# A fused attention and int8 feed-forward layer on eight cores: the weighted-sum matmuls trail the scores by six key blocks instead of four, and the weight transfers lose `single_packet`

## The chip, the cores and the metric

The kernel runs on all 8 cores of one Trainium2 chip. Every core runs the same program on its own share of the tokens, and there is no exchange between cores. The metric is the device time in microseconds of the slowest core, lower is better. A difference of 2% is about 63 us here.

## The reference, cut to what matters

```python
x = x + attn(layernorm(x), Wq, Wk, Wv, memory, memory_norm, memory_weight)   # 4 x 2048 x 2048
x = x + ffn(layernorm(x), w_gate, w_up, w_down, s_gate, s_up, s_down)

# attn: 32 query heads of 64, 8 key/value heads
probs = softmax(einsum('bsqhd,bthd->bqhst', qh, kh) / 8)
a_dot = einsum('bqhst,bthd->bsqhd', probs, vh)
sigma_q = elu(q);  a_mem = sigma_q @ memory / (sigma_q @ memory_norm)
out = a_dot * (1 - w) + a_mem * w                  # w = sigmoid(memory_weight)

# ffn: 2048 -> 8192 -> 2048, int8 weights with a scale per output column
out = ((silu((x @ w_gate) * s_gate) * ((x @ w_up) * s_up)) @ w_down) * s_down
```

Four sequences of 2048 tokens lie over eight cores: a core computes keys and values for a whole sequence (2048 tokens) and queries, attention and the feed-forward for 1024 of them.

## The kernel before, in words

The program is one function, `build_nc`. A small planner (`Plan.do`) appends each instruction to its engine's list in the order of the source and puts the semaphore waits in front of it; nothing is reordered, so the order of the loops is the order on each engine. `"t"` is TensorE, `"v"` VectorE, `"s"` ScalarE, `"y"` SyncE and `"g"` GpSimd. Every weight is loaded by a DMA that GpSimd issues, since it also casts (f32 or int8 in HBM, bf16 in SBUF); GpSimd waits for a buffer to come free, issues, and goes on.

1. Layer norm of the 16 token tiles and the projections: `wvb` (L179) is loaded once, the query weights in 16 pieces (L345), the key weights in 4 pieces twice (L361).
2. Then two passes `p` over 512 queries each. A pass has three stages.
   - Attention (L443 to L519). The loop `i2` runs over 16 pairs of heads. For each pair, 16 key blocks `tc` of 128 keys are worked through. A score step is two matmuls, L454 into `pAB` for one head and L461 into `pCD` for the other, each into one of two halves (`half`), so scores of block `tc` wait for the exponentials of block `tc - 2`. ScalarE then does two exponentials of 128 x 512 (L474) into `A_et`, a ring of 8 slots per head. The weighted sum of a block (L486, "AV" below: one matmul into `pE`, one into `pF`) is issued four steps after its scores; it accumulates over all 16 blocks. So the loop over `tc` has 20 steps: the first four have scores alone, the last four have AV alone. When the last AV is done, VectorE copies `pE` and `pF` out (L494, L498, L507, L514), and the first AV of the next pair waits for that. An exponential also waits for the AV that read its ring slot 8 blocks before.
   - The memory term and the sum of both (L528 to L648), mainly VectorE.
   - The feed-forward, for two groups `grp` of 256 tokens. First 64 steps `it` of gate (L698, 16 matmuls of 256 columns), up (L707, the same) and, two steps behind, the down projection of the group's first 128 tokens (L669, 4 matmuls of 512 columns). `wgb`, `wub` and `wdb` have two buffers each, and a step takes three transfers of 512 KB (written size): L688, L693, L663. Then the down projection of the second 128 tokens (L767), which reads all of `w_down` again through six buffers (L761), 64 transfers for 256 matmuls. These 64 steps are called the second down pass below; it comes four times in the program, as do the gate/up stages.

The first lines of the attention step's AV part:

```python
if tc >= 4:
    tca = tc - 4
    for st in range(2):
        ...
        waits=[t_exp[(j, tca)], war_av[st] if tca == 0 else None]
```

Of the kernel before, what the change touches and what calls it, by code (L numbers as in the profile page):

```python
# [59 lines left out]
def build_nc():  # L60
# [3 lines left out]
    wqt_d = nc.dram_tensor("wqt", [16, 128, 2048], F32, kind="ExternalInput").ap()  # L64
# [21 lines left out]
    with es:  # L86
# [72 lines left out]
        P = Plan()  # L159
# [16 lines left out]
            t_consts = P.do("y", lambda e, d=dst, s=src: e.dma_start(out=d[:], in_=s[:]), stream="c")  # L176
        t_mem = P.do("g", lambda e: e.dma_start(out=mem_s[:], in_=mem_d[:]), stream="m")
        t_mem = P.do("g", lambda e: e.dma_start(out=mnorm[:], in_=mnorm_d[:]), stream="m")
        t_wv = P.do("g", lambda e: e.dma_start(out=wvb[:], in_=wvt_d[:].rearrange("p (c f) -> p c f", f=512), single_packet=True), stream="wv")  # L179

        t_w1 = P.do("s", lambda e: e.activation(wcol[:, 0:1], mw_s[:], AF.Sigmoid),
                    waits=[t_consts], inc=True)
# [143 lines left out]
        for H in range(2):  # L326
            for i8 in range(8):
                i = H * 8 + i8
                sl = i % 2
                t_x[i] = P.do("y", lambda e, i=i, sl=sl: e.dma_start(  # L330
                    out=xstage[:, sl, :], in_=x_d[i * 128:(i + 1) * 128, :]),
                    waits=[war_xstage[sl]], stream="xs%d" % sl)
                tv3 = emit_ln_stats(xstage[:, sl, :], sl, [t_x[i]], war_lnst[sl],
                                    sum_on_s=True)
                if i8 > 0:
                    emit_tile_tail(i - 1)
                t_apply[i] = emit_ln_apply(xstage[:, sl, :], sl, tv3, eng="g")
                war_xstage[sl] = t_apply[i]
            emit_tile_tail(H * 8 + 7)
            t_half[H] = t_tile[H * 8 + 7]  # L340

            if H == 0:
                for j in range(16):
                    wb = j % 2
                    t_wq[j] = P.do("g", lambda e, j=j, wb=wb: e.dma_start(  # L345
                        out=wgb[wb][:], in_=wqt_d[j].rearrange("p (c m) -> p c m", m=128),
                single_packet=True),
                        waits=[war_wbuf[wb]], stream="wg%d" % wb)
                    for sc in range(2):
                        tv = qkv_group(  # L350
                            lambda c, j=j, wb=wb: wgb[wb][:, c, :],
                            lambda c, sc=sc: A_ln[:, c, sc * 512:(sc + 1) * 512],
                            lambda e, bank, j=j, sc=sc: e.tensor_copy(
                                q_fm[:, j, sc * 512:(sc + 1) * 512], bank[:, 0:512]),
                            16, [t_wq[j], t_tile[4 * sc + 3]])
                    t_q_evac[j] = tv
                    war_wbuf[wb] = ("t", P.cnt["t"])
                    norm_q_chunk(j)
            for j2 in range(4):
                wb = j2 % 2  # L360
                t_wk = P.do("g", lambda e, j2=j2, wb=wb: e.dma_start(  # L361
                    out=wgb[wb][:], in_=wkt_d[j2].rearrange("p (c m) -> p c m", m=128),
                single_packet=True),
                    waits=[war_wbuf[wb]], stream="wg%d" % wb)
                for tcH in range(2):
                    tv = qkv_group(
                        lambda c, wb=wb: wgb[wb][:, c, :],
                        lambda c, tcH=tcH: A_ln[:, c, tcH * 512:(tcH + 1) * 512],
                        lambda e, bank, j2=j2, H=H, tcH=tcH: e.tensor_copy(
                            k_fm[:, j2, H * 1024 + tcH * 512: H * 1024 + (tcH + 1) * 512],  # L370
                            bank[:, 0:512]),
                        16, [t_wk, t_tile[H * 8 + tcH * 4 + 3]])
                t_k_evac[(j2, H)] = tv
                war_wbuf[wb] = ("t", P.cnt["t"])
                norm_k_chunk(j2, H, tv)
            if H == 0:
                t_k0_done = ("t", P.cnt["t"])
            t_qkv_done[H] = ("t", P.cnt["t"])
# [37 lines left out]
        for p in range(2):  # L416
# [26 lines left out]
            for i2 in range(16):  # L443
                prs = (2 * i2, 2 * i2 + 1)
                kc = (2 * i2) % 8 // 2
                for tc in range(20):
                    if tc < 16:
                        half = (tc % 2) * 512
                        w0 = [t_exp.get((prs[1], tc - 2)), t_bias,
                              war_arena_p2]  # L450
                        if i2 == 0 and tc < 2:
                            w0 += war_sb_init[tc % 2]
                        ttSA = P.do("t", lambda e, i2=i2, kc=kc, tc=tc, half=half, p=p:
                                    e.matmul(pAB[0:128, half:half + 512],  # L454
                                             k_fm[0:64, kc, tc * 128:(tc + 1) * 128],
                                             q_fm[0:64, i2, p * 512:(p + 1) * 512],
                                             start=True, stop=True,
                                             tile_position=(0, 0)),
                                    waits=w0, inc=True)
                        ttSB = P.do("t", lambda e, i2=i2, kc=kc, tc=tc, half=half, p=p:  # L460
                                    e.matmul(pCD[0:128, half:half + 512],  # L461
                                             k_fm[64:128, kc, tc * 128:(tc + 1) * 128],
                                             q_fm[64:128, i2, p * 512:(p + 1) * 512],
                                             start=True, stop=True,
                                             tile_position=(64, 0)),
                                    inc=True)
                        for st in range(2):
                            j = prs[st]
                            wslot = t_av.get((j, tc - 8))
                            if wslot is None and i2 > 0:  # L470
                                wslot = t_av.get((j - 2, tc + 8))
                            t_exp[(j, tc)] = P.do(
                                "s", lambda e, j=j, tc=tc, st=st, half=half:
                                e.activation(A_et[:, st * 8 + tc % 8, :],  # L474
                                             sbank[st][0:128, half:half + 512],
                                             AF.Exp, bias=bias_s[:, j:j + 1],
                                             scale=0.125),
                                waits=[ttSB, t_bias, wslot,
                                       war_arena_p2], relax=True, inc=True)
                    if tc >= 4:  # L480
                        tca = tc - 4
                        for st in range(2):
                            j = prs[st]
                            t_av[(j, tca)] = P.do(
                                "t", lambda e, j=j, tca=tca, st=st:
                                e.matmul(avbank[st][0:65, 0:512],  # L486
                                         v_tm[:, tca, j % 8, 0:65],
                                         A_et[:, st * 8 + tca % 8, :],
                                         start=(tca == 0), stop=(tca == 15)),
                                waits=[t_exp[(j, tca)],  # L490
                                       war_av[st] if tca == 0 else None],
                                inc=True)
# [162 lines left out]
            for grp in range(2):  # L655
# [4 lines left out]
                def emit_down0(ic, grp=grp):  # L660
                    sl = ic % 2
                    buf = wdb[sl]
                    t_wd = P.do("g", lambda e, ic=ic, buf=buf: e.dma_start(  # L663
                        out=buf[:], in_=wd_d[ic * 128:(ic + 1) * 128, :],
                        single_packet=True),
                        waits=[ttdn0.get(ic - 2), war_wd[sl] if ic < 2 else None],
                        stream="wd%d" % sl)
                    for dch in range(4):
# [14 lines left out]
                for it in range(64):  # L683
                    wb = it % 2
                    wu_extra = [t_qkv_done[1]] if (p == 0 and grp == 0 and it < 2) else []
                    if it < 2:
                        wu_extra = wu_extra + [war_wu_reg[wb]]
                    t_wg = P.do("g", lambda e, it=it, wb=wb: e.dma_start(  # L688
                        out=wgb[wb][:], in_=wg_d[it], single_packet=True),
                        waits=[war_wbuf[wb]] +  # L690
                              ([war_wg_reg[wb]] if it < 2 else []),
                        stream="wd%d" % (4 + wb) if False else "wg%d" % wb)
                    t_wu = P.do("g", lambda e, it=it, wb=wb: e.dma_start(  # L693
                        out=wub[wb][:], in_=wu_d[it], single_packet=True),
                        waits=[war_wbuf[wb]] + wu_extra, stream="wu%d" % wb)
                    ttg = None
                    for c in range(16):
# [60 lines left out]
                for ic in range(64):  # L758
                    sl = ic % 6
                    buf = wd_slots[sl]  # L760
                    t_wd = P.do("g", lambda e, ic=ic, buf=buf: e.dma_start(  # L761
                        out=buf[:], in_=wd_d[ic * 128:(ic + 1) * 128, :],
                        single_packet=True),
                        waits=[ttdn.get(ic - 6), war_wd6[sl] if ic < 6 else None],
                        stream="wd%d" % sl)
                    for dch in range(4):
# [127 lines left out]
```

How the kernel before makes its waits and increments, by code:

```python
            def run(eng):  # L801
                for item in stream:
                    if item[0] == "w":
                        eng.wait_ge(sems[item[1]], item[2])
                    elif item[0] == "i":
                        item[1](eng).then_inc(sems[item[2]], STEP[item[2]])
                    else:
                        item[1](eng)
```

## Time and profile before

| what | us |
|---|---|
| median of the runs shown (two: 3134.87 and 3320.86) | 3227.86 |
| the profiled execution | 3137.72 |
| its span, first to last instruction of the slowest core (core 3) | 3136.2 |
| spans of the eight cores | 3120.4 to 3136.2 |
| core 3: one attention stage of 16 head pairs (two in the program) | about 326 |
| core 3: one second down pass of 64 steps (four in the program) | about 82 |

Rows of the profile are in microseconds from the span's start unless they say ns. PE is TensorE's matmuls, PEld its weight loads, DVE VectorE, ACT ScalarE, POOL GpSimd, SP SyncE. A row of the timeline reads: start, duration, engine, line, operation, what is written <- what is read, count, and in brackets how long the engine was idle before and what ended that. Matmuls overlap: what one costs is the distance between two starts, not its duration.

### The profile page before, as it was taken

How to read it: one execution, taken by the hardware profiler on the slowest of the kernel's cores; microseconds unless marked ns; L12 is line 12 of the kernel's file. 1: busy time of each engine (PE TensorE's matmuls, PEld its weight loads, DVE VectorE, ACT ScalarE, POOL GpSimd, SP SyncE). 2: the span in 40 equal slices, each digit the busy share in tenths (PEclk: the TensorE clock that was granted, in tenths of full speed). 3: DMA queues.
4: the chain of work that ended last, by engine and by line, in shares of the span. 5: the costliest groups of instructions: out<-in, count | busy, mean ns of one | idle time of the engine just before them, and what ended most of it. 6: DMA issues, size and time to landing. Idle time of an engine off the chain costs nothing.

```text
span 3136.2 us, 40984 instructions; the slowest of 8 cores (3120.4 to 3136.2 us)
## 1 busy us (share of the span) xinstructions
PE 2445.5 (78%) x14265; PEld 1329.0 (42%) x14265; DVE 595.7 (19%) x1657; ACT 963.5 (31%) x1671; POOL 590.6 (19%) x1071
## 2 busy tenths in 40 slices
PE   3777666878744799968999778875449997799986
PEld 1223222222211577725778222221127774277752
DVE  2332333111136200020000011112550002000010
ACT  2200030999920122201222059995002221022210
POOL 1100010000000233323333310000003332333333
PEclk9788778888855799989999988887559998999999
DMA  4222214000000599979999960000009996999999
GB/s 116 74 44 44 44 65 121 4 4 4 4 1 1 187 358 359 350 280 366 357 348 361 361 218 4 3 4 3 1 28 353 351 354 248 395 339 361 349 338 346
DMA packets 161916, 591.77 MB, mean 189 GB/s; under 512 B 20920, under 2 KB 23096, under 8 KB 157368
## 3 DMA queue, kind: packets, MB, share of 16 engines
q0 software_dynamic: 151344, 552.14, 51.5%
q1 hardware_dynamic: 10376, 37.01, 3.4%
q8 instruction: 124, 2.03, 0.3%
q14 instruction: 72, 0.59, 0.1%
HBM read 325.23 MB, written 8.39 MB: 106 GB/s over the span
## 4 chain that ended last, share of the span: by engine, by line
PE 56%; DMA 12%; DVE 12%; ACT 11%; issue 8%; DVEq 1%; SPq 0%; POOL 0%; ACTq 0%; POOLq 0%
PE pAB L707 13%; PE pAB L698 13%; ACT arena L474 9%; DMA warena<-wd 8%; PE pCD L296 5%; PE pAB L296 4%; PE pCD L669 3%; PE pE L486 3%; PE pAB L454 3%; DMA warena<-wg 2%; PE pF L486 2%; PE pAB L571 2%; PE pT L238 2%; PE pF L669 2%; PE pE L669 2%
## 5 line engine op out<-in xcount | busy, mean ns | idle before, releaser
L698 PE MATMUL pAB<-ln_fm,warena 128*128 128x256 bf16 x4096 | 493.7, 274 | 13.4 <-DMA warena<-wg 11.1
L707 PE MATMUL pAB<-ln_fm,warena 128*128 128x256 bf16 x4096 | 490.0, 273 | 10.3 <-DMA warena<-wu 6.1
L688 POOL DMA_DIRECT2D warena<-wg x256 | 136.2, 532 | 1733.0 <-PE pAB L698 1037.2
L698 PEld LDWEIGHTS pAB<-ln_fm,warena 128*128 128x128 bf16 x4096 | 398.6, 98 | 125.6 <-issue 41.9
L707 PEld LDWEIGHTS pAB<-ln_fm,warena 128*128 128x128 bf16 x4096 | 399.3, 98 | 63.9 <-issue 16.9
L474 ACT ACTIVATE arena<-pAB,bias_s 128x512 bf16<-128x512 f32 x512 | 373.2, 729 | 46.1 <-PE pCD L461 41.9
L474 ACT ACTIVATE arena<-pCD,bias_s 128x512 bf16<-128x512 f32 x512 | 375.5, 733 | 0.0
L454 PE MATMUL pAB<-q_fm,k_fm 64*128 64x512 bf16 x512 | 217.2, 434 | 134.7 <-ACT arena L474 129.8
L714 ACT ACTIVATE gtmp<-pAB,sg_s 128x256 bf16<-128x256 f32 x256 | 121.4, 474 | 567.1 <-PE pAB L707 504.1
L722 DVE TENSOR_TENSOR arena<-gtmp,utmp 128x256 bf16<-128x256 bf16 x256 | 75.0, 293 | 1063.8 <-ACT utmp L718 1063.8
L486 PE MATMUL pE<-arena,v_tm 128*65 128x512 bf16 x512 | 228.0, 445 | 0.0
L461 PE MATMUL pCD<-q_fm,k_fm 64*128 64x512 bf16 x512 | 222.2, 444 | 0.0
L718 ACT ACTIVATE utmp<-pAB,su_s 128x256 bf16<-128x256 f32 x256 | 121.4, 474 | 321.9 <-PE pAB L707 318.9
L767 PE MATMUL pCD<-warena,arena 128*128 128x512 bf16 x512 | 158.4, 390 | 77.6 <-DMA warena<-wd 65.9
L486 PE MATMUL pF<-arena,v_tm 128*65 128x512 bf16 x512 | 216.8, 423 | 0.0
L238 PE MATMUL pT<-eyeb_s,lnstage 128*128 128x128 bf16 x384 | 78.2, 248 | 167.4 <-DVE arena L241 68.3
L454 PEld LDWEIGHTS pAB<-q_fm,k_fm 64*128 64x128 bf16 x512 | 46.1, 95 | 370.7 <-issue 370.7
L761 POOL DMA_DIRECT2D warena<-wd x256 | 135.5, 531 | 250.4 <-PE pF L767 151.0
L669 PE MATMUL pCD<-warena,arena 128*128 128x512 bf16 x512 | 153.1, 381 | 16.1 <-DMA warena<-wd 15.7
L663 POOL DMA_DIRECT2D warena<-wd x256 | 141.6, 553 | 37.8 <-PE pAB L698 16.4
L693 POOL DMA_DIRECT2D warena<-wu x256 | 139.4, 544 | 41.3 <-PE pF L279 16.3
L494 DVE CAST arena<-pE 64x512 bf16<-64x512 f32 x32 | 21.9, 683 | 560.3 <-PE pE L486 560.3
(118 smaller groups left out, 2074.4 us busy)
## 6 DMA issues: line engine op xcount, KB each, us to landing
warena<-wd POOLq DMA_DIRECT2D x512, 512.0 KB, 6.0
warena<-wg POOLq DMA_DIRECT2D x256, 512.0 KB, 3.9
warena<-wu POOLq DMA_DIRECT2D x256, 512.0 KB, 4.8
xstage<-x SPq DMA_DIRECT2D x16, 1024.0 KB, 5.0
warena<-wqt POOLq DMA_DIRECT2D x16, 512.0 KB, 5.2
x<-x SPq DMA_DIRECT2D x8, 1024.0 KB, 13.5
y<-x SPq DMA_DIRECT2D x8, 1024.0 KB, 4.7
warena<-wkt POOLq DMA_DIRECT2D x8, 512.0 KB, 5.2
```

What stands on the lines that cost most here:

```text
L238: tt = P.do("t", lambda e, c=c, ap=ap: e.transpose(ap, lnstage[:, slot, c * 128:(c + 1) * 128], eyeb[:]), waits=[t_apply, tslot_war[si]] + ...
L296: tt = P.do("t", lambda e, c=c, bank=bank: e.matmul(bank[:, 0:512], lhs_fn(c), rhs_fn(c), start=(c == 0), stop=(c == nK - 1)), waits=(wait ...
L454: e.matmul(pAB[0:128, half:half + 512], k_fm[0:64, kc, tc * 128:(tc + 1) * 128], q_fm[0:64, i2, p * 512:(p + 1) * 512], start=True, stop=True,
L461: e.matmul(pCD[0:128, half:half + 512], k_fm[64:128, kc, tc * 128:(tc + 1) * 128], q_fm[64:128, i2, p * 512:(p + 1) * 512], start=True, st ...
L474: e.activation(A_et[:, st * 8 + tc % 8, :], sbank[st][0:128, half:half + 512], AF.Exp, bias=bias_s[:, j:j + 1], scale=0.125),
L486: e.matmul(avbank[st][0:65, 0:512], v_tm[:, tca, j % 8, 0:65], A_et[:, st * 8 + tca % 8, :], start=(tca == 0), stop=(tca == 15)),
L663: t_wd = P.do("g", lambda e, ic=ic, buf=buf: e.dma_start(out=buf[:], in_=wd_d[ic * 128:(ic + 1) * 128, :], single_packet=True), waits=[ttd ...
L669: ttdn0[ic] = P.do("t", lambda e, ic=ic, buf=buf, dch=dch: e.matmul(dbanks[dch][0:128, 0:512], A_fu[:, ic, 0:128], buf[:, dch * 512:(dch + ...
L693: t_wu = P.do("g", lambda e, it=it, wb=wb: e.dma_start(out=wub[wb][:], in_=wu_d[it], single_packet=True), waits=[war_wbuf[wb]] + wu_extra, ...
L698: ttg = P.do("t", lambda e, it=it, wb=wb, c=c: e.matmul(pA[0:128, 0:256], wgb[wb][:, c, :], ln2_fm[:, c, 0:256], start=(c == 0), stop=(c = ...
L707: ttu = P.do("t", lambda e, it=it, wb=wb, c=c: e.matmul(pB[0:128, 0:256], wub[wb][:, c, :], ln2_fm[:, c, 0:256], start=(c == 0), stop=(c = ...
L767: ttdn[ic] = P.do("t", lambda e, ic=ic, buf=buf, dch=dch: e.matmul(dbanks[dch][0:128, 0:512], A_fu[:, ic, 128:256], buf[:, dch * 512:(dch ...
```

## The change

Two things. In the attention loop AV trails the scores by six steps instead of four: the loop has 22 steps, the first six with scores alone and the last six with AV alone. And the flag `single_packet=True` is taken off all weight transfers (`wvb`, L345, L361, L663, L688, L693, L761: 1,049 DMAs); what they move, who issues them and what they wait for stays.

```diff
-        t_wv = P.do("g", lambda e: e.dma_start(out=wvb[:], in_=wvt_d[:].rearrange("p (c f) -> p c f", f=512), single_packet=True), stream="wv")
+        t_wv = P.do("g", lambda e: e.dma_start(out=wvb[:], in_=wvt_d[:].rearrange("p (c f) -> p c f", f=512)), stream="wv")
...
-                for tc in range(20):
+                for tc in range(22):
...
-                    if tc >= 4:
-                        tca = tc - 4
+                    if tc >= 6:
+                        tca = tc - 6
...
                     t_wg = P.do("g", lambda e, it=it, wb=wb: e.dma_start(
-                        out=wgb[wb][:], in_=wg_d[it], single_packet=True),
+                        out=wgb[wb][:], in_=wg_d[it]),
...
                     t_wu = P.do("g", lambda e, it=it, wb=wb: e.dma_start(
-                        out=wub[wb][:], in_=wu_d[it], single_packet=True),
+                        out=wub[wb][:], in_=wu_d[it]),
...
                     t_wd = P.do("g", lambda e, ic=ic, buf=buf: e.dma_start(
-                        out=buf[:], in_=wd_d[ic * 128:(ic + 1) * 128, :],
-                        single_packet=True),
+                        out=buf[:], in_=wd_d[ic * 128:(ic + 1) * 128, :]),
```

The change moves instructions on TensorE alone. The first place is the start of a head pair other than the first. In the kernel before, TensorE has this order from the fourth score step on (`k_fm` and `q_fm` are keys and queries, `arena` holds the exponentials, `v_tm` the values):

```order
L454 MATMUL pAB<-q_fm,k_fm 128x512 [waits sem_s]
L461 MATMUL pCD<-q_fm,k_fm 128x512
L454 MATMUL pAB<-q_fm,k_fm 128x512 [waits sem_s]
L461 MATMUL pCD<-q_fm,k_fm 128x512
L486 MATMUL pE<-arena,v_tm 65x512 [waits sem_v]
L486 MATMUL pF<-arena,v_tm 65x512 [waits sem_v]
```

In the changed kernel, from the same score step on (L454 is L452 there, L461 is L459, L486 is L484):

```order
L452 MATMUL pAB<-q_fm,k_fm 128x512 [waits sem_s]
L459 MATMUL pCD<-q_fm,k_fm 128x512
L452 MATMUL pAB<-q_fm,k_fm 128x512 [waits sem_s]
L459 MATMUL pCD<-q_fm,k_fm 128x512
L452 MATMUL pAB<-q_fm,k_fm 128x512 [waits sem_s]
L459 MATMUL pCD<-q_fm,k_fm 128x512
L452 MATMUL pAB<-q_fm,k_fm 128x512 [waits sem_s]
L459 MATMUL pCD<-q_fm,k_fm 128x512
L484 MATMUL pE<-arena,v_tm 65x512 [waits sem_v]
L484 MATMUL pF<-arena,v_tm 65x512 [waits sem_v]
```

The first AV, which waits for VectorE's copies of the pair before, comes behind two more score steps.

The second place is the end of a head pair: the last score step, the AVs behind it and the first score matmul of the next pair. Before:

```order
L454 MATMUL pAB<-q_fm,k_fm 128x512 [waits sem_s]
L461 MATMUL pCD<-q_fm,k_fm 128x512
L486 MATMUL pE<-arena,v_tm 65x512
L486 MATMUL pF<-arena,v_tm 65x512
...
L486 MATMUL pE<-arena,v_tm 65x512 [waits sem_s]
L486 MATMUL pF<-arena,v_tm 65x512 [waits sem_s]
L486 MATMUL pE<-arena,v_tm 65x512 [waits sem_s]
L486 MATMUL pF<-arena,v_tm 65x512 [waits sem_s]
L454 MATMUL pAB<-q_fm,k_fm 128x512
```

In the changed kernel, where the "..." also stands for rows like the two above it:

```order
L484 MATMUL pE<-arena,v_tm 65x512
L484 MATMUL pF<-arena,v_tm 65x512
...
L484 MATMUL pE<-arena,v_tm 65x512 [waits sem_s]
L484 MATMUL pF<-arena,v_tm 65x512 [waits sem_s]
L484 MATMUL pE<-arena,v_tm 65x512 [waits sem_s]
L484 MATMUL pF<-arena,v_tm 65x512 [waits sem_s]
L452 MATMUL pAB<-q_fm,k_fm 128x512
```

Between the last score matmul (L461) and the next pair's first (L454) stood 10 AV matmuls, and now 14 stand there. The last four wait for ScalarE in both.

## Rows read from the trace of the kernel before

**Rows 1.** The page: busy time of each engine, and the granted clock in 40 slices

```profile
PE 2445.5 (78%) x14265; PEld 1329.0 (42%) x14265; DVE 595.7 (19%) x1657; ACT 963.5 (31%) x1671; POOL 590.6 (19%) x1071
PEclk9788778888855799989999988887559998999999
```

**Rows 2.** The page: the chain that ended last, by line

```profile
PE pAB L707 13%; PE pAB L698 13%; ACT arena L474 9%; DMA warena<-wd 8%; PE pCD L296 5%; PE pAB L296 4%; PE pCD L669 3%; PE pE L486 3%; PE pAB L454 3%; DMA warena<-wg 2%; PE pF L486 2%; PE pAB L571 2%; PE pT L238 2%; PE pF L669 2%; PE pE L669 2%
```

**Rows 3.** Windows: stretch and length, busy us (instructions) by engine, granted clock, DMA share, GB/s

```profile
545.40:872.20 326.80, 259.93 (x1020) 72.28 (x1020) 41.14 (x60) 303.44 (x513) 0.00 (x0) 0.85 0.02 4
648.50:668.10 19.60, 14.39 (x66) 4.44 (x64) 2.76 (x5) 18.63 (x33) 0.00 (x0) 1.00 0.02 5
671.15:677.98 6.83, 6.17 (x18) 1.24 (x18) 0.00 (x0) 6.19 (x11) 0.00 (x0) 0.50 0.03 7
```

**Rows 4.** Timeline around the end of one head pair

```profile
645.36 0.37 PE L454 MATMUL pAB<-q_fm,k_fm 64*128 64x512 bf16 x1 [0.21 <-ACT arena L474]
...
645.68 0.41 PE L486 MATMUL pE<-arena,v_tm 128*65 128x512 bf16 x1
...
646.71 0.81 ACT L474 ACTIVATE arena<-pCD,bias_s 128x512 bf16<-128x512 f32 x1
...
647.43 0.38 PE L486 MATMUL pE<-arena,v_tm 128*65 128x512 bf16 x1
647.67 0.38 PE L486 MATMUL pF<-arena,v_tm 128*65 128x512 bf16 x1
...
647.98 0.39 PE L454 MATMUL pAB<-q_fm,k_fm 64*128 64x512 bf16 x1
...
648.50 0.69 ACT L474 ACTIVATE arena<-pAB,bias_s 128x512 bf16<-128x512 f32 x1 [0.97 <-PE pCD L461]
```

**Rows 5.** Timeline of VectorE: the copy that ends a head pair, three in a row

```profile
647.92 0.68 DVE L494 CAST arena<-pE 64x512 bf16<-64x512 f32 x1 [17.51 <-PE pE L486]
...
667.50 0.68 DVE L494 CAST arena<-pE 64x512 bf16<-64x512 f32 x1 [16.54 <-PE pE L486]
...
688.22 0.68 DVE L494 CAST arena<-pE 64x512 bf16<-64x512 f32 x1 [17.67 <-PE pE L486]
```

**Rows 6.** Timeline: first AV of a pair, score steps at half and at full clock

```profile
672.34 0.64 PE L486 MATMUL pE<-arena,v_tm 128*65 128x512 bf16 x1
...
674.88 0.60 PE L454 MATMUL pAB<-q_fm,k_fm 64*128 64x512 bf16 x1
...
676.41 0.60 PE L454 MATMUL pAB<-q_fm,k_fm 64*128 64x512 bf16 x1
...
682.19 0.37 PE L454 MATMUL pAB<-q_fm,k_fm 64*128 64x512 bf16 x1 [0.21 <-ACT arena L474]
...
683.34 0.37 PE L454 MATMUL pAB<-q_fm,k_fm 64*128 64x512 bf16 x1 [0.21 <-ACT arena L474]
```

**Rows 7.** The second down pass: its DMA issues (duration in ns), and one PE row

```profile
L761 POOL DMA_DIRECT2D warena<-wd x58: 527/527/539, 1366.1 to 1439.5; - x58
...
1437.96 0.59 PE L767 MATMUL pCD<-warena,arena 128*128 128x512 bf16 x2 [0.26 <-DMA warena<-wd]
```

**Rows 8.** DMA issues of the page: KB each, median us from issue to landing

```profile
warena<-wd POOLq DMA_DIRECT2D x512, 512.0 KB, 6.0
...
warena<-wkt POOLq DMA_DIRECT2D x8, 512.0 KB, 5.2
...
mem_s<-memi POOLq DMA_DIRECT2D x1, 512.0 KB, 6.3
```

**Rows 9.** Gate/up stage: a wg transfer's issue, matmuls of two steps, and median landing

```profile
1103.79 0.53 POOL L688 DMA_DIRECT2D warena<-wg  x1 [2.77 <-PE pCD L669]
...
1103.95 1.91 PE L698 MATMUL pAB<-ln_fm,warena 128*128 128x256 bf16 x16
...
1108.30 1.91 PE L698 MATMUL pAB<-ln_fm,warena 128*128 128x256 bf16 x16
...
warena<-wg POOLq DMA_DIRECT2D x22, 512.0 KB, 3.7
```

More of the change, by code:

```diff
@@ L345, in build_nc @@
                     t_wq[j] = P.do("g", lambda e, j=j, wb=wb: e.dma_start(
-                        out=wgb[wb][:], in_=wqt_d[j].rearrange("p (c m) -> p c m", m=128),
-                single_packet=True),
+                        out=wgb[wb][:], in_=wqt_d[j].rearrange("p (c m) -> p c m", m=128)),
                         waits=[war_wbuf[wb]], stream="wg%d" % wb)
@@ L361, in build_nc @@
                 t_wk = P.do("g", lambda e, j2=j2, wb=wb: e.dma_start(
-                    out=wgb[wb][:], in_=wkt_d[j2].rearrange("p (c m) -> p c m", m=128),
-                single_packet=True),
+                    out=wgb[wb][:], in_=wkt_d[j2].rearrange("p (c m) -> p c m", m=128)),
                     waits=[war_wbuf[wb]], stream="wg%d" % wb)
@@ L663, in emit_down0 @@
                     t_wd = P.do("g", lambda e, ic=ic, buf=buf: e.dma_start(
-                        out=buf[:], in_=wd_d[ic * 128:(ic + 1) * 128, :],
-                        single_packet=True),
+                        out=buf[:], in_=wd_d[ic * 128:(ic + 1) * 128, :]),
                         waits=[ttdn0.get(ic - 2), war_wd[sl] if ic < 2 else None],
@@ L761, in build_nc @@
                     t_wd = P.do("g", lambda e, ic=ic, buf=buf: e.dma_start(
-                        out=buf[:], in_=wd_d[ic * 128:(ic + 1) * 128, :],
-                        single_packet=True),
+                        out=buf[:], in_=wd_d[ic * 128:(ic + 1) * 128, :]),
                         waits=[ttdn.get(ic - 6), war_wd6[sl] if ic < 6 else None],
```

## The prediction, made before the changed kernel ran

> **What bounds the kernel now.** I read the page first, then the chain, and then the stages that the change touches one by one. The busy shares [rows 1] say little by themselves: TensorE is busy 78% of the span, but that is a mean over stages with different limits. The clock digits already show that there is something to look for: in the slices of attention (8 to 11 and 24 to 28 of 40) TensorE is granted 0.7 to 0.8 of its clock, 0.85 as the mean of the first stage [rows 3], not the full one. The chain [rows 2] names the parts: gate and up matmuls 26%, the exponentials of attention (L474) 9%, and transfers of w_down 8%, some 250 us. So the two edits touch two different bounds. The later AV touches a stage in which ScalarE leads, and the flag touches a stage that waits for DMA.
>
> **Attention, the bound inside a head pair.** At the full clock a step takes 683.34 - 682.19 = 1.15 us [rows 6], and TensorE was idle 0.21 us before its scores, released by ScalarE: ScalarE's two exponentials set the pace. Within a pair that ran at the full clock ScalarE was busy 18.63 of 19.60 us [rows 3]. What is left, about 1 us, is the hole at the pair's end [rows 4]: ScalarE starts its last exponential at 646.71, and the first of the next pair starts at 648.50, after 0.97 us of idleness ended by a score matmul. Who fills the time between? TensorE starts the last score at 645.36, its first AV at 645.68 and the ninth at 647.43. That is 1.75 us for 8 matmuls, 0.219 each, with no gap; the tenth follows at 647.67 and the next pair's scores at 647.98. The last exponential ended at 647.52 (646.71 + 0.81), before the tenth AV started. So the tail behind the last score is bound by the number of matmuls that stand in it, not by the exponentials, although it is close: 0.15 us.
>
> **The tail, first term.** The change puts four more AV matmuls behind the last score (14, not 10). All AVs that were deferred have their exponentials ready, so nothing hides them: during them ScalarE finishes its last two steps, as before, and then it has no scores to work on. The steps before cannot absorb them either, since TensorE runs its list in order. Cost per pair: 4 x 0.219 = 0.88 us; for 2 x 16 pairs 28 us. The bound from below is the 0.15 us that might be covered if I misread the end of the last exponential: 32 x 0.73 = 23 us. From above, at half the clock a 512-column matmul would cost twice as much, 56 us, but the tail stood at the full clock in the pairs I looked at: the half-clock stretch is early in the pair, 671.15 to 677.98 [rows 3], after the copy at 667.50 and before the one at 688.22 [rows 5]. I take 28.
>
> What else the six steps could wait for: an exponential needs its ring slot free, that is the AV of 8 blocks before. With a delay of 6 that AV is issued two steps before the exponential, ahead of the exponential's own scores on the same engine, so it adds no wait. The first AV of a pair waits for VectorE's copies; it comes two steps later now, which can only help, and nothing was waiting there.
>
> **The clock, second term.** The period of a pair is read from the copies that end it [rows 5]: 19.58 us for the pair that the second row ends, 20.72 for the next. The difference is the clock. The first pair was granted 1.00 throughout, the second 0.50 (1.2 GHz) from 671.15 to 677.98 [rows 3]. In that stretch a step takes 676.41 - 674.88 = 1.53 us instead of 1.15 [rows 6], since two scores together and two AVs at half speed are more than two exponentials. The fall comes after a stretch in which TensorE had only scores to do. The whole first stage has 16 pairs in about 325.5 us (326.8 less 1.3 around it), 20.34 each, or 0.76 above 19.58; two stages lose 32 x 0.76 = 24 us to the clock.
>
> What do two more steps with scores alone do to this? Steps without AV do not suffer from the half clock. If the low stretch stayed where it is, it would fall on steps without AV, and up to 24 us would come back; that is the lower bound, -24. But the rise at 677.98 came only after AVs had run for 5.6 us (the first AV of that pair starts at 672.34 [rows 6]); if the rise follows the AVs, it moves two steps too, and the same three slow steps stand there, later. The pairs that now escape the fall would no longer do so, since the light stretch is longer. The upper bound is two more slow steps per pair, 32 x 2 x 0.38 = +24. I take +6, nearer to "it moves along" than to either end.
>
> The Trainium skill's page "TensorE: Matmul & The Clock Gate", in "Part 1: The HAM clock gate", says that the throttled state is the default and that activity releases it. The trace agrees: 0.50 follows the steps with scores alone. By this rule the longer light stretch makes the low clock certain in every pair, and does not by itself shorten it.
>
> **The flag, third term.** Nothing is moved on GpSimd's list, no byte is added and no wait changes. What the flag could touch is how fast a transfer runs, how long it takes to land, and how long GpSimd takes to issue it. The second down pass is where it would show at once: 58 issues from 1366.1 to 1439.5 [rows 7], 1.29 us for each 512 KB or 407 GB/s, while TensorE's 4 matmuls of 512 columns need 4 x 0.219 = 0.88 us. It waits for the DMA in each step, 0.26 us in the row shown. Four passes of 64 steps are 330 us, and each per cent of transfer rate is 3.3 us. The gate/up stage has a step of 1108.30 - 1103.95 = 4.35 us [rows 9] for three transfers, 3 x 1.29 = 3.87 us at that rate: 11% in hand. Of latency there is less in hand: wg issued at 1103.79 is wanted at 1108.30, 4.51 us later, and lands after 3.7, which leaves 0.8.
>
> No row shows the same transfer with and without the flag. The nearest is mem_s, a 512 KB casting load that never had it: 6.3 us to landing against 5.2 for the key weights that had it [rows 8], with a cold start and the small constants beside it. So the upper bound: 1.1 us later landing in all. In gate/up 1.1 - 0.8 = 0.3 us a step, 256 steps, 77 us; in the second down pass six buffers are in flight (6 x 1.29 = 7.7 us against 6.0 + 1.1 to land), little more, say 15: +92 us. The lower bound is a pass that no longer waits: 256 x (1.29 - 0.88) = -105 us, if the DMA were suddenly that fast. Both are far off. I take the value of the rows in which each descriptor's work is unchanged, one per cent of the passes, +3 us.
>
> The Trainium skill's page "DMA: Bandwidth & Descriptors", in "Why small descriptors are slow (HBM only)", gives a packet a fixed overhead of about 3 cycles beside one cycle per 32 bytes, and says that packing descriptors together is only worth it up to 256 bytes. The rows here have 4 KB written per partition; by the page that is 3 in 131 cycles, an estimate of 2.3%, or 8 us of 330. No row of this trace shows it. With it the sum would be 5 us higher.
>
> **The sum.** The profiled execution took 3137.7 us, 1.5 more than its span. 3137.7 + 28 + 6 + 3 = 3174.7, so 3175 us, 1.2% above it. The median of the two runs shown is 3227.86, between 3134.87 and 3320.86; my sum stands to the lower of them, which the profiled execution matches within 3 us. A difference of 2% is about what a measurement of this kernel can tell from no change.
>
> **The rivals.**
> *A, not slower: the clock pays for the tail.* The half-clock stretch comes where it comes now, over steps that no longer have AVs, and is over when they begin. Then the 24 us are gained back against the 28 of the tail: 3137.7 + 28 - 24 + 0 = 3142. For it: the fall comes early, about 3.6 us after the pair's end. Against it: the rise followed the AVs. It decides if the granted clock rises before the seventh step.
> *B, the rate drops.* Transfers lose 10%: the second down passes go from 1.29 to 1.42 us a step, +33, while gate/up still hides it (3 x 1.42 = 4.26 under 4.35). 3137.7 + 34 + 33 = 3205. For it: those passes have no reserve. Against it: nothing in rows says that splitting costs as much.
> *C, the landing gets later.* The upper bound above, 3137.7 + 34 + 92 = 3264. For it: mem_s, and only 0.8 us in hand at wg. Against it: mem_s was the first transfer of all.
> *D, the flag does nothing.* If the transfers were cut the same way in both kernels, only attention moves: 3172. It is inside my forecast.
>
> **How the numbers follow.** Forecast, D included, 0.66; A 0.12; B 0.12; C 0.10. The forecast by itself spans 3155 to 3195 (first term 23 to 28, second -5 to +20, third 0 to 10, and a few us of scatter). The range is 3143 to 3212: it takes in B and most of A and leaves C and a part of A out. 2% above 3137.7 is 3200.5: slower by over 2% is C, half of B and a little of the forecast's upper edge, 0.17. Faster by over 2% would need the lower bound of the flag, 0.03. Within 2%: 0.80.
>
> **What would show it.** Right, step by step: ScalarE's idle time before the first exponential of a pair grows from 0.97 to about 1.85 us; pairs at the full clock take 20.4 to 20.5 us between copies; nearly every pair has a stretch at 0.50, which ends some 2 us later in the pair than now; an attention stage takes about 343 us instead of 326. The second down pass keeps 1.29 us a step, and wg still lands within 4 us in gate/up. The prediction is wrong if the attention stage stays within 5 us of 326 (A, or a tail that is hidden), or if the steps of the second down pass or the landing times grow by more than 3% (B, C).

## The result, and the profile after

The changed kernel takes 3166.31 us (median of 11 runs) against 3142.67 us for the kernel before (median of 10). The ratio to the kernel before is 1.0083, with a 95% interval of 1.0070 to 1.0097: 26 us slower. The ratio leaves out the executions in which the cores of a die showed a lower granted clock and took over 1% longer (three of the 10, one of the 11), so it gives 26 us where the two medians lie 24 apart. The prediction was 3175 us, 1.2% above the profiled execution of before (3137.7). It set aside the median of two runs, 3227.86 us, that was shown before it, and nothing below goes by that either.

Against the profiled execution the sign and the place were right; the size was 37 us where 26 came. The page of the profile after first, whose slowest core is core 4:

```profile
span 3166.1 us, 40808 instructions; the slowest of 8 cores (3142.4 to 3166.1 us)
...
PEclk8788867788865699989999988887559998999999
...
PE pAB L704 14%; PE pAB L695 13%; ACT arena L472 9%; DMA warena<-wd 8%; PE pCD L296 5%; PE pAB L296 5%; PE pE L484 3%; PE pCD L666 3%; PE pAB L452 3%; PE pF L484 3%; PE pAB L569 2%; DMA warena<-wg 2%; PE pT L238 2%; PE pF L666 2%; PE pE L666 2%
```

The chain has the same members with the same shares as [rows 2]: the transfers of w_down are at 8% in both. The page cannot tell where 26 us went. The two stages of attention can. In windows of core 4 (length, busy us of PE, PEld, DVE, ACT and POOL, granted clock, DMA share, GB/s):

```profile
557.50:896.10 338.60, 257.80 (x1019) 74.68 (x1018) 41.15 (x60) 303.29 (x513) 0.00 (x0) 0.83 0.02 4
...
669.70:676.50 6.80, 6.18 (x18) 1.24 (x18) 0.00 (x0) 6.15 (x11) 0.00 (x0) 0.50 0.01 2
...
1857.10:2195.00 337.90, 257.36 (x1018) 74.71 (x1019) 44.55 (x65) 303.01 (x513) 0.00 (x0) 0.83 0.07 23
```

Each stage is about 338 us long, 326.8 before [rows 3], with the same busy time of ScalarE (303 us). ScalarE is not slower, it waits more. The clock is granted at 0.83 instead of 0.85. The end of a pair in the timeline, to be held beside [rows 4]:

```profile
660.30 0.37 PE L452 MATMUL pAB<-q_fm,k_fm 64*128 64x512 bf16 x1 [0.21 <-ACT arena L472]
...
660.63 0.41 PE L484 MATMUL pE<-arena,v_tm 128*65 128x512 bf16 x1
...
661.67 0.80 ACT L472 ACTIVATE arena<-pCD,bias_s 128x512 bf16<-128x512 f32 x1
...
663.46 0.38 PE L484 MATMUL pF<-arena,v_tm 128*65 128x512 bf16 x1
...
663.77 0.39 PE L452 MATMUL pAB<-q_fm,k_fm 64*128 64x512 bf16 x1
...
664.29 0.69 ACT L472 ACTIVATE arena<-pAB,bias_s 128x512 bf16<-128x512 f32 x1 [1.82 <-PE pCD L459]
```

From the last score at 660.30 the 14 AVs run without a gap to 663.46, and ScalarE, whose last exponential started at 661.67, is idle 1.82 us until the next pair's first scores: 0.97 before. In what follows "the hole" is the distance between the start of a pair's last exponential and the start of the next pair's first, here 664.29 - 661.67 = 2.62 us. Inside a stretch of exponentials the same distance is 0.57. The hole of before [rows 4] is 648.50 - 646.71 = 1.79.

The transfers show nothing. The issues of the second down pass (as in [rows 7]), the median landing of wg in gate/up (as in [rows 9]), and from the page the pieces in which the weight queue moved its data:

```profile
L758 POOL DMA_DIRECT2D warena<-wd x52: 527/527/530, 1400.3 to 1465.6; - x52
```

```profile
warena<-wg POOLq DMA_DIRECT2D x22, 512.0 KB, 3.9
```

```profile
DMA packets 161916, 591.77 MB, mean 187 GB/s; under 512 B 20920, under 2 KB 23096, under 8 KB 157368
## 3 DMA queue, kind: packets, MB, share of 16 engines
q0 software_dynamic: 151344, 552.14, 50.9%
```

65.3 us for 51 steps is 1.28 us a step, 1.29 before. And wg lands after 3.9 us in the stretch where it was 3.7; over the eight cores it is 3.7 to 3.9 in both. The number of pieces is the same as before, where the page has 161916 in all and 151344 on this queue too.

One table holds what the later sections use. Each value is worked out from the starts of all exponentials in the timelines of all eight cores (of the run with three steps, cores 0 to 3 alone): the hole as the mean of 30 per core, and "within a pair" as the time from its first exponential to its last, the mean of 32 per core. At the full clock throughout, within a pair would be 15 steps of 1.145 us and one distance of 0.57, 17.75 us. Whatever is above that is lost to the half clock.

| kernel | AV matmuls behind the last score | first AV at step | hole, us | within a pair, us | ratio to before |
|---|---|---|---|---|---|
| two steps | 6 | 2 | 1.84 | 18.15 | 0.9965 (0.9950 to 0.9980) |
| three steps | 8 | 3 | 1.83 | 18.21 | 0.9979 (0.9948 to 1.0009) |
| before, four steps | 10 | 4 | 1.79 | 18.63 | 1 |
| five steps | 12 | 5 | 2.18 | 18.31 | 1.0016 (1.0001 to 1.0031) |
| changed kernel, six steps | 14 | 6 | 2.60 | 18.59 | 1.0083 (1.0070 to 1.0097) |
| seven steps | 16 | 7 | 3.01 | 18.62 | 1.0139 (1.0115 to 1.0163) |
| late start, short tail | 10 | 6 | 1.87 | 18.65 | 1.0004 (0.9991 to 1.0017) |
| early start, long tail | 14 | 4 | 2.64 | 18.29 | 1.0046 (1.0031 to 1.0061) |
| pipelined | none | 6 | 0.57 | 18.28 | 0.9843 (0.9825 to 0.9862) |
| pipelined, five steps | none | 7 | 0.57 | 18.23 | 0.9829 (0.9806 to 0.9852) |

Steps are counted from 0 in this table, as `tc` is. The changed kernel against the one before: hole +0.81, within a pair -0.04. With 30 holes and 32 pairs that is 23 us. The tail behind the last pair of each of the two stages is not followed by a hole in this count; at the same price, an estimate, it adds 2 us, so that 25 of the 26 us have their place.

### The profile page after: what moved, and what is told of

It is laid out like the page before. It is cut to its first block, busy times and chain, and to the rows that moved or that the text cites. A ratio compares the mean times of both kernels' runs of the same rounds, so it can differ in the third digit from the quotient of the medians.

```text
span 3166.1 us, 40808 instructions; the slowest of 8 cores (3142.4 to 3166.1 us)
## 1 busy us (share of the span) xinstructions
PE 2427.0 (77%) x14089; PEld 1336.0 (42%) x14265; DVE 595.7 (19%) x1657; ACT 962.0 (30%) x1671; POOL 590.6 (19%) x1071
## 2 busy tenths in 40 slices
DMA packets 161916, 591.77 MB, mean 187 GB/s; under 512 B 20920, under 2 KB 23096, under 8 KB 157368
## 3 DMA queue, kind: packets, MB, share of 16 engines
q0 software_dynamic: 151344, 552.14, 50.9%
## 4 chain that ended last, share of the span: by engine, by line
PE 57%; DVE 11%; DMA 11%; ACT 11%; issue 8%; DVEq 1%; SPq 0%; ACTq 0%; POOL 0%; POOLq 0%
PE pAB L704 14%; PE pAB L695 13%; ACT arena L472 9%; DMA warena<-wd 8%; PE pCD L296 5%; PE pAB L296 5%; PE pE L484 3%; PE pCD L666 3%; PE pAB L452 3%; PE pF L484 3%; PE pAB L569 2%; DMA warena<-wg 2%; PE pT L238 2%; PE pF L666 2%; PE pE L666 2%
## 5 line engine op out<-in xcount | busy, mean ns | idle before, releaser
L452 PE MATMUL pAB<-q_fm,k_fm 64*128 64x512 bf16 x512 | 222.7, 445 | 164.1 <-ACT arena L472 157.0
L459 PE MATMUL pCD<-q_fm,k_fm 64*128 64x512 bf16 x512 | 228.2, 456 | 0.0
L484 PE MATMUL pE<-arena,v_tm 128*65 128x512 bf16 x512 | 223.3, 436 | 0.0
L763 PE MATMUL pCD<-warena,arena 128*128 128x512 bf16 x500 | 155.2, 389 | 81.1 <-DMA warena<-wd 68.1
L484 PE MATMUL pF<-arena,v_tm 128*65 128x512 bf16 x512 | 215.9, 422 | 0.0
L452 PEld LDWEIGHTS pAB<-q_fm,k_fm 64*128 64x128 bf16 x512 | 46.4, 95 | 397.8 <-issue 397.8
L666 PE MATMUL pCD<-warena,arena 128*128 128x512 bf16 x388 | 125.9, 380 | 21.6 <-DMA warena<-wd 15.1
```

The lines of the kernel that those rows point to most:

```text
L452: e.matmul(pAB[0:128, half:half + 512], k_fm[0:64, kc, tc * 128:(tc + 1) * 128], q_fm[0:64, i2, p * 512:(p + 1) * 512], start=True, stop=True,
L459: e.matmul(pCD[0:128, half:half + 512], k_fm[64:128, kc, tc * 128:(tc + 1) * 128], q_fm[64:128, i2, p * 512:(p + 1) * 512], start=True, st ...
L484: e.matmul(avbank[st][0:65, 0:512], v_tm[:, tca, j % 8, 0:65], A_et[:, st * 8 + tca % 8, :], start=(tca == 0), stop=(tca == 15)),
L666: ttdn0[ic] = P.do("t", lambda e, ic=ic, buf=buf, dch=dch: e.matmul(dbanks[dch][0:128, 0:512], A_fu[:, ic, 0:128], buf[:, dch * 512:(dch + ...
L763: ttdn[ic] = P.do("t", lambda e, ic=ic, buf=buf, dch=dch: e.matmul(dbanks[dch][0:128, 0:512], A_fu[:, ic, 128:256], buf[:, dch * 512:(dch ...
```

## The experiments

### The two edits apart

The later AV alone, from the kernel before:

```diff
-                for tc in range(20):
+                for tc in range(22):
...
-                    if tc >= 4:
-                        tca = tc - 4
+                    if tc >= 6:
+                        tca = tc - 6
```

> The later weighted sum alone; single_packet stays on all weight transfers. Theory T (the four further AV matmuls in each pair's tail carry the whole loss, the flag nothing): as the changed kernel, ratio to before 1.008 (within 0.002), hole before a pair's first exponential 2.6 us between starts. Rival F (the flag has a share, the tail less): ratio clearly under the changed kernel's 1.0083, for a share of a third 1.0055. Rival G (the flag's removal gave some time back): ratio over 1.010.

Measured: ratio 1.0066 (1.0049 to 1.0083), hole 2.60 us, within a pair 18.58. By the trace the attention stages are those of the changed kernel (336.3 us from the first to the last exponential's start against 336.5, the mean over eight cores, and 324.9 in the kernel before). The ratio alone would leave room for a small share of the flag. So the flag alone, the changed kernel with the loop of before:

```diff
-                        out=wgb[wb][:], in_=wg_d[it], single_packet=True),
+                        out=wgb[wb][:], in_=wg_d[it]),
```

and likewise at all other weight transfers, so that against the kernel before only the flag differs.

> The flag alone: no single_packet on any weight transfer, AV four steps behind as before. Theory T: ratio 1.000 within 0.0015, the second down pass at 1.29 us a step and 407 GB/s, wg landing 3.7 to 3.9 us after issue in gate/up. Rival F: ratio 1.003 or more (8 us), seen as a longer step of the second down pass, since it waits for its transfers in every step. Rival G: ratio under 0.998.

Measured: ratio 1.0004 (0.9992 to 1.0015), hole 1.79 us. The second down pass on core 0 of this run:

```profile
L758 POOL DMA_DIRECT2D warena<-wd x39: 527/527/530, 1399.6 to 1449.2; - x39
...
DMA to landing us min/median/max: 6.0/6.0/6.9
```

49.6 us for 38 steps, 1.305 us, with a landing of 6.0 us as in [rows 8] and 527 ns for an issue as in [rows 7]. One pass on one core is a small sample; from the seventh to the last issue, over all four passes and eight cores, the step is 1.300 us before and 1.297 us in this run. This is the stage that waits for its transfers in every step, so a slower or later transfer could not hide here. Rivals F and G are out: the flag is worth nothing that can be measured, between -2.5 and +4.7 us (0.08% and 0.15% of 3138).

### Late start or long tail

The change did two things in each pair: the first AV came later, and more AVs stood behind the last score. The next two kernels do one each, by a table that says which blocks' AVs stand at a step.

```diff
-                    if tc >= 4:
-                        tca = tc - 4
-                        for st in range(2):
+                    for tca in AVS[tc]:
+                        for st in range(2):
```

Late start, short tail: one AV pair a step from step 6 on, two at steps 12 and 14, so that the last four steps are those of before.

> From the kernel before: the first AV of a pair comes at the seventh step, as in the changed kernel, but steps 12 and 14 hold two AVs each, so that 10 AV matmuls stand behind the last score, as in the kernel before. Theory T: the tail is all, so ratio 1.000 within 0.002; hole between exponentials 1.78 us as before; the stretch at half the clock costs about 0.75 us a pair as in both kernels. Rival S (the late start costs, by longer low clock and a later first AV, the tail is hidden): ratio as the changed kernel, 1.008. If ScalarE is held up by the steps with two AVs: up to 0.1 us each, 2 x 32 x 0.1 = 6 us, ratio 1.002.

Measured: ratio 1.0004 (0.9991 to 1.0017), hole 1.87, within a pair 18.65. The first AV stands where the changed kernel has it, and nothing that the ratio can tell is lost. Rival S is out. The hole is 0.08 us longer than before, where 1.78 was expected, which is 2 to 3 us in all. What the catching up costs by itself was not measured, since the time within a pair (+0.02) also holds what the clock does.

Early start, long tail: one AV pair a step from step 4 on, none at steps 10 and 14, 22 steps in all.

> The counterpart: the first AV at the fifth step, as in the kernel before, but steps 10 and 14 hold none, so that 14 AV matmuls stand behind the last score, as in the changed kernel. Theory T: 32 x 0.82 = 26 us, ratio 1.0083 within 0.002, hole 2.60 us. Rival S: ratio 1.000, hole 1.78 us.

Measured: ratio 1.0046 (1.0031 to 1.0061), hole 2.64. The hole is what theory T said, 0.85 us more than before, or 27 us. The time is not, and the ratio is outside the 1.0083 within 0.002 that was expected: within a pair it took 18.29 us, 0.34 less than before, and that gives 11 of the 27 us back. The granted clock of the first attention stage on core 3, in windows of the kernel before and of this one, shows where it came from:

```profile
546.00:872.00 326.00, 259.73 (x1019) 72.17 (x1019) 41.14 (x60) 302.84 (x513) 0.00 (x0) 0.86 0.02 4
```

```profile
546.00:872.00 326.00, 242.28 (x999) 72.41 (x998) 41.16 (x60) 294.01 (x501) 0.00 (x0) 0.91 0.02 4
```

So the tail costs what theory T says, and the half clock is a second account that moves by itself. A ratio alone would have been read as "half a tail".

### How the hole goes with the number of steps

The kernel before with 2, 3, 5 and 7 steps between scores and AV, the edit being the one above with other numbers.

> AV two steps behind the scores, flags as before: 6 AV matmuls behind the last score instead of 10, and only two steps with scores alone. Theory T (the hole is the number of AV matmuls behind the last score, down to where the last exponential ends it): the hole shrinks by 0.15 us alone, from 1.79 to 1.64, since the last exponential ends 0.15 us before the last AV starts; 5 us in all. Theory C (what is lost to the half clock, 18.63 us within a pair against 17.8 at the full clock, hangs on how long TensorE has scores alone): fewer pairs fall, time within a pair under 18.4, so together 12 to 32 us, ratio 0.990 to 0.996. Rival L (the half clock comes with the hole itself, and a later or earlier AV changes nothing): low time as before, ratio 0.998.

> AV three steps behind: 8 AV matmuls behind the last score. Theory T: hole 1.64 us, as with two steps, since it is the last exponential that ends it from here on. Theory C: between the kernel before and the two-step one, ratio 0.993 to 0.998. Rival L: ratio 0.998.

> AV five steps behind, order of the pairs as before: 12 AV matmuls behind the last score. Theory T with what the runs with two and three steps showed (a floor near 1.8 us, from the last exponential through the last AV to the next scores, which the kernel before just meets): the hole is 1.79 + 0.41 = 2.20 us, half of the changed kernel's loss, ratio 1.004. Rival (the tail costs only from the sixth step on): hole 1.8 us, ratio 1.000.

> AV seven steps behind: 16 AV matmuls behind the last score. Theory T: 0.43 us more than the changed kernel in each hole, 3.03 us; against the kernel before 32 x 1.24 = 40 us, ratio 1.0125 if the clock costs the same as in both. Rival (the hole is not proportional, the changed kernel's step was a threshold): hole near 2.6 us, ratio 1.008.

Measured, from the table: 1.84, 1.83, 1.79, 2.18, 2.60, 3.01 us for 2, 3, 4, 5, 6, 7 steps. From four steps on, each adds 0.39 to 0.42 us, a little under two AV matmuls at 0.219 us each; the changed kernel's two steps are no threshold. Below four the hole does not shrink. I had expected 1.64 us there, and that was a miss. The two-step kernel's timeline on core 3 says why:

```profile
652.93 0.94 ACT L474 ACTIVATE arena<-pCD,bias_s 128x512 bf16<-128x512 f32 x1
653.44 0.38 PE L486 MATMUL pE<-arena,v_tm 128*65 128x512 bf16 x1 [0.20 <-ACT arena L474]
...
654.02 0.38 PE L486 MATMUL pF<-arena,v_tm 128*65 128x512 bf16 x1 [0.20 <-ACT arena L474]
654.33 0.39 PE L454 MATMUL pAB<-q_fm,k_fm 64*128 64x512 bf16 x1
...
654.85 0.69 ACT L474 ACTIVATE arena<-pAB,bias_s 128x512 bf16<-128x512 f32 x1 [0.97 <-PE pCD L461]
```

Here the last AVs do wait, each released by ScalarE: the last starts 1.09 us after the last exponential (654.02 - 652.93), and from there it is 0.31 to the next scores and 0.52 more to the next exponential, 1.92 us in this pair. This AV starts 0.15 us after the recorded end of the exponential that releases it (652.93 + 0.94 = 653.87). That is the 0.15 us that I saw between 647.52 and 647.67 in [rows 4]: they were no slack, but the time from an exponential's end to the AV that waited for it. In the mean over all holes it is 0.14 to 0.15 us in the kernels with two, three and four steps, and 0.55, 0.99 and 1.42 us with five, six and seven. Four steps are just where the two bounds meet: up to there the last exponential sets the end of the pair, with more steps the AVs in line.

Of the ratios, that of seven steps (1.0139) is near the 1.0125 expected, which its interval holds. Five steps gave 1.0016 where 1.004 was expected, and its interval ends at 1.0031: the hole is as forecast, but 0.32 us a pair came back from the clock (18.31 us against 18.63). Two steps gave 0.9965. Of the 14 us that its two columns make (32 x (0.48 - 0.05)), all come from the clock. Theory C was right in sign there and just short of its range, which ended at 0.996. Three steps gave a ratio whose interval holds 1 and most of the expected range, so it decides nothing. Rival L expected 0.998, which the interval of the two-step run just reaches; it is out by the time within a pair, 18.15 us with two steps and 18.63 before, which by L would be the same.

### A version without a tail

If the tail is the cost, it can be taken out: the scores of the next pair are issued between the last four AV steps of this one. The first AV of a pair stands at step 6 and the steps 12 and 14 hold two, as in the kernel with the late start. Only the last pair of a stage still has a tail.

```diff
-                for tc in range(20):
+                for tc in range(16 if i2 < 15 else 20):
...
-                        w0 = [t_exp.get((prs[1], tc - 2)), t_bias,
+                        w0 = [t_exp.get((prs[1], tc - 2)) or t_exp.get((prs[1] - 2, tc + 14)), t_bias,
...
+                    todo = [(i2, a) for a in AVS.get(tc, [])]
+                    if i2 > 0 and tc < 16:
+                        todo = [(i2 - 1, a) for a in AVS.get(tc + 16, [])] + todo
+                    for (ia, tca) in todo:
+                        emit_av(ia, tca)
+                        if tca == 15:
+                            emit_copies(ia)
```

> The scores of the next pair are issued between the last AVs of this one, so that no tail is left: the pair's last four AVs stand at steps 0 to 3 of the next pair, its first AV at step 6 (VectorE's copies, 3 us, lie between), and steps 12 and 14 hold two. Theory T: the hole goes from 1.79 us to the ordinary distance of 0.57, 30 x 1.22 = 37 us, ratio 0.988. Theory C on top: TensorE is never long with scores alone, so the half clock mostly goes and up to 0.8 us a pair comes back, 25 us, ratio 0.980. Rival V (VectorE's copies hold the first AV and, behind it, the scores): a new hole of up to 1 us at step 6, ratio 0.992 or more.

Measured: ratio 0.9843 (0.9825 to 0.9862), 49 us faster than the kernel before, and so faster than both kernels of the change. The hole is 0.57 us, the ordinary distance. The timeline around the copies (in this kernel L521 is the exponential, L501 the first score matmul, L450 the AV and L461 to L481 the copies):

```profile
645.83 0.68 DVE L461 CAST arena<-pE 64x512 bf16<-64x512 f32 x1 [15.96 <-PE pE L450]
646.15 0.37 PE L501 MATMUL pAB<-q_fm,k_fm 64*128 64x512 bf16 x1 [0.21 <-ACT arena L521]
646.32 0.85 ACT L521 ACTIVATE arena<-pCD,bias_s 128x512 bf16<-128x512 f32 x1
646.54 0.69 DVE L465 COPY rsrow<-pE 1x512 f32<-1x512 f32 x1
646.88 0.85 ACT L521 ACTIVATE arena<-pAB,bias_s 128x512 bf16<-128x512 f32 x1
...
648.18 0.69 DVE L481 COPY rsrow<-pF 1x512 f32<-1x512 f32 x1
...
648.78 0.41 PE L450 MATMUL pE<-arena,v_tm 128*65 128x512 bf16 x1
...
649.03 0.38 PE L450 MATMUL pF<-arena,v_tm 128*65 128x512 bf16 x1
```

While VectorE empties `pE` and `pF` from 645.83 on, the exponentials go on at 0.56 us apart, and TensorE is idle between scores, released by ScalarE. The next pair's first AV into `pE` starts at 648.78, well after the last copy of `pE` has ended (646.54 + 0.69 = 647.23), and the one into `pF` at 649.03, just after the last copy of `pF` has (648.87). Rival V did not come about. Theory T's part was met (37 us); of theory C's 25 us some 11 came (32 x 0.35), since within a pair it still takes 18.28 us.

The same order with AV five steps behind at a pair's end:

> The pipelined order with AV five steps behind at a pair's end and its first AV at step 7, one step later than in the first pipelined kernel. Theory T (the delay costs nothing but the tail, and there is no tail here): hole 0.57 us and ratio 0.984 within 0.002, as with four steps. Rival (the delay itself costs, wherever the AVs stand): 30 x 0.41 = 12 us more, ratio 0.988.

Measured: ratio 0.9829 (0.9806 to 0.9852), hole 0.57. The rival's 0.988 is outside the interval. Without a tail between pairs, a longer delay costs nothing. That is the sharpest form of theory T: it is not the delay that costs, but the AVs that stand alone at the end of a pair.

## Why the prediction was right or wrong

**What bounds each stage.** Right. Attention is led by ScalarE, and its loss is the hole at a pair's end. The second down pass is led by its transfers.

**The tail, +28 us.** Right as a mechanism, shown by the runs with a long tail alone, with a short tail alone and with 5 and 7 steps. It measured +0.81 us in each hole, 26 us for 32 tails. I had priced four more matmuls at 0.219 us each, 0.88 in all. From the first AV to the last it was 1.99 us before (645.68 to 647.67) and is 2.83 us now (660.63 to 663.46), 0.84 more: the last pair of AVs, which waited a little for its exponential before (647.43 to 647.67, 0.24), no longer does. The misread slack of 0.15 us did not enter the value, only the lower bound; the short delays showed that there was none.

**The clock, +6 us.** This is the step that failed: it measured 32 x (18.59 - 18.63), -1 us. Two things in it were right. No pair escapes any longer: 23 of the 256 pairs (32 on each of eight cores) had no stretch at half the clock before, and none is without one now. And the slow steps moved with the AVs: in the mean over pairs and cores the steps well above 1.15 us are 4 to 6 before (1.37, 1.48 and 1.48 us) and 6 to 8 after (1.46, 1.50 and 1.32). What was wrong is "if the rise follows the AVs, it moves two steps too, and the same three slow steps stand there". The first AV of a pair moved by 2.36 us, from 4.22 to 6.58 us after the pair's first exponential; the rise of the clock moved by only 1.33 us, from 9.23 to 10.56, so that it came 4.0 us after the first AV instead of 5.0. The stretch at half the clock grew, from 6.0 to 7.2 us a pair, but the steps without AV, which stay at 1.14 to 1.16 us in the mean, took the added part of it and more. Counting steps longer than 1.3 us, a pair that had any had 2.9 of them before and has 2.7 now. This gain made up for the pairs that no longer escape. By the granted clock of the windows a stage stood at half the clock for 2 x (1 - 0.85) x 326.8 = 98 us before and for 2 x (1 - 0.83) x 338.6 = 115 us after, and yet lost no more time. Why the rise moved by less than the AVs is not shown.

**The flag, +3 us.** The other mis-sized term, with no row that gave its size: it measured 0.0004 (-0.0008 to +0.0015), 1 us most likely, and zero for all that can be told. What I took from the nearest rows was an allowance, not a reading, and the row on which the upper bound rested (mem_s, 6.3 us) said nothing of the flag. The changed kernel's page has 5.2 us for the key weights, now without the flag, as in [rows 8].

**The sum.** 3137.7 + 26 - 1 + 0 = 3163 us; the profiled execution took 3167.7 and the median is 3166.3. All three errors, 2, 7 and 3 us, had the same sign, which turned 0.8% into 1.2%. The remaining 3 to 5 us are in the starting point: the profiled execution lies 5 us under the median of before. The prediction took 2% for what a measurement of this kernel can tell; the interval of the ratio is 0.15% to either side here, so that 0.8% is clear of it.

**The rivals.** A would have needed the rise before the seventh step. It comes after it in every pair of all eight cores, as at 676.50 in the window above, in a pair whose first exponential started at 664.29 (A's sum of 3142 also lay just outside the stated range, not mostly inside it). B and C fall with the flag run: the step and the landing are those of before. D, the flag does nothing, is what happened, and its condition fits the page: the pieces are the same in number with and without the flag. It stood inside the forecast at 3172, closer than the 3175 that was given.

**The signs named beforehand.** The idle time before a pair's first exponential: 1.85 us forecast, 1.82 seen. An attention stage: about 343 us forecast, 338 seen. Nearly every pair with a stretch at half the clock, ending some 2 us later: seen in every pair, and ending 9.1 to 12.3 us after the pair's first exponential in the first stage of core 4 against 8.7 to 9.9 on core 3 before; in the mean over all cores that is 1.3 us later and not 2. Pairs at the full clock with 20.4 to 20.5 us between copies: there are none left to look at. The second down pass at 1.29 us: 1.28 seen.

## What to carry to other kernels

When two engines run in step with a delay between them, the delay is paid where the pipeline is emptied: count what the leading engine waits for behind its last item, and multiply by the number of times it is emptied. If that happens often, here 32 times, do not tune the delay but issue the next group's first items between this group's last ones; that was worth 1.6% where the change of delay was worth -0.8%. And before a transfer's flag is given a price, find the stage that waits for its transfers in every step and read its step: if it does not move there, there is little reason to expect it elsewhere.

## What the runs showed of the hardware that was not expected

- Without `single_packet` a casting load of 512 KB, 4 KB per partition, issues in the same 527 ns, lands in the same 6.0 us and runs at the same 1.28 to 1.31 us a step, some 400 GB/s written, on a core of a chip whose eight cores all run this program. The Trainium skill's page "DMA: Bandwidth & Descriptors", in "Why small descriptors are slow (HBM only)", gives a fixed cost to each packet, from which 2.3% was estimated for cutting these loads up. By the profile's records the loads are cut the same way in both kernels, 151344 pieces on their queue, 134272 of them (128 for each of the 1,049 loads) of 4096 bytes, and a piece of 4096 bytes takes 187 ns in the mean over all cores in both. So that cost had nothing to act on here, and the runs say nothing about its size. Whether the flag joins pieces in a way that these records do not show is open.
- What the half clock costs does not rise or fall steadily with the length of the stretch of scores alone. Within a pair it took 18.15, 18.21, 18.63, 18.31, 18.59 and 18.62 us for 2 to 7 steps: the kernel before sits on a worse value than its neighbour with five steps. With the start of before and the longer tail it was 18.29. Why four steps are worse than five was not settled; that it hangs on where in the pair the fall comes is a guess and not shown.
- An AV matmul that waits for an exponential starts 0.15 us after the exponential's recorded end and 1.09 us after its start (two steps, 654.02 - 652.93), while exponentials follow each other every 0.57 us.
